# Attention and FFN on one core: three shared PSUM banks, normalising on VectorE, one output step per batch, new engine orders, and q, k, v as three float32r products

## The reference, cut to what matters

```python
xn = layernorm(x)                                   # x: 8 batches x 256 tokens x 256
kqv = xn @ Wqkv + bqkv                              # 16 heads of 16
scores = einsum('bsnh,btnh->bnst', k, q) / 4        # triu kept, -10000 below the diagonal
attn = softmax(scores, axis=2)
out = einsum('bnkq,bknh->bqnh', attn, v) @ Wo + bo
x_qdq = fp8(clip(xn / s_in, -448, 448)) * s_in
ffn = x_qdq @ (w_fp8 * w_scale).T
result = x + out + ffn                              # float32
```

## Time and profile before

| | us |
|---|---|
| median of 2 runs | 283.17 (281.4 and 284.94) |
| the profiled execution, its own time | 286.0 |
| its span, first to last instruction | 284.3 |
| TensorE matmuls busy | 205.1 (72%) |
| VectorE, ScalarE, GpSimd busy | 139.2, 104.1, 155.1 |
| mean granted TensorE clock | 0.862 of 2.4 GHz |

### The profile page before, as it was taken

How to read it: one execution, slowest core, us unless ns; L and a number is a source line. 1 busy time by engine, 2 the same in 40 slices (tenths; PEclk the granted TensorE clock), 3 DMA queues, 4 the chain that set the end, 5 groups by cost and what they waited for, 6 DMA issues and landing times.

```text
span 284.3 us, 4678 instructions
## 1 busy us (share of the span) xinstructions
PE 205.1 (72%) x1668; PEld 154.0 (54%) x1668; DVE 139.2 (49%) x265; ACT 104.1 (37%) x171; POOL 155.1 (55%) x352
## 2 busy tenths in 40 slices
PE   5196633847886597968785779766987869958945
PEld 5175532636755285746463656655765646635613
DVE  3836832567766144747671164529454743421220
ACT  4122300323530444246424434154416524635410
POOL 7472394496482866458737936386627433443320
PEclk9997965865995977999999697999799986986977
DMA  6619939759282006520661025703370010010011
GB/s 162 180 26 202 200 69 158 207 95 122 59 140 36 0 0 113 101 58 1 111 117 40 2 60 96 112 0 68 71 127 2 5 39 0 6 37 0 2 37 37
DMA packets 24444, 20.59 MB, mean 72 GB/s; under 512 B 2589, under 2 KB 24166, under 8 KB 24422
## 3 DMA queue, kind: packets, MB, share of 16 engines
q1 hardware_dynamic: 23024, 19.18, 35.9%
q10 hardware_dynamic: 1398, 1.12, 1.5%
HBM read 3.22 MB, written 2.10 MB: 19 GB/s over the span
## 4 chain that ended last, share of the span: by engine, by line
PE 51%; DVE 19%; POOL 14%; issue 8%; ACT 6%; DMA 1%; DVEq 0%; POOLq 0%; ACTq 0%
PE bankB L917 8%; PE ps L864 6%; PE bankA L978 5%; DVE row_max L661 5%; PE pso L889 5%; POOL xn L258 4%; ACT probs L473 3%; POOL probs L387 3%; PE bankB L924 3%; PE ps L847 2%; PE ps L843 2%; PE ps L849 2%; PE pso L895 2%; PE bankB L907 2%; PE bankA L924 2%
## 5 line engine op out<-in xcount | busy, mean ns | idle before, releaser
L661 DVE TENSOR_REDUCE row_max<-ps 128x4 f32<-128x1024 f32 (+1 forms) x48 | 58.5, 1221 | 64.7 <-PE ps L849 35.9
L387 POOL TENSOR_SCALAR_AFFINE_SELECT probs<-probs 128x256 f32<-128x256 f32 x128 | 49.1, 413 | 49.9 <-ACT probs L473 49.7
L473 ACT ACTIVATE probs<-ps 128x1024 f32<-128x1024 f32 x48 | 49.1, 1023 | 18.3 <-PE ps L864 13.8
L864 PE MATMUL ps<-q_stack,k_stack 99*128 99x256 bf16 x128 | 23.9, 319 | 11.6 <-ACT probs L473 11.6
L405 POOL TENSOR_TENSOR y<-y,x_all 128x256 f32<-128x256 f32 x16 | 11.2, 724 | 33.9 <-ACT y L528 33.9
L917 PE MATMUL bankB<-xT,wqk_sb 128*128 128x256 f32 x64 | 22.4, 511 | 8.0 <-ACT xs L522 7.9
L847 PE MATMUL ps<-k_stack,q_stack 96*128 96x128 bf16 x128 | 21.4, 244 | 6.5 <-DVE row_max L661 6.3
L864 PEld LDWEIGHTS ps<-q_stack,k_stack 99*128 99x128 bf16 x128 | 13.1, 113 | 18.6 <-ACT probs L473 14.6
L917 PEld LDWEIGHTS bankB<-xT,wqk_sb 128*128 128x128 f32 x64 | 16.3, 267 | 11.8 <-issue 7.3
L849 PE MATMUL ps<-k_stack,q_stack 125*128 125x128 bf16 x128 | 21.4, 243 | 0.0
L495 ACT ACTIVATE o_raw<-pso 128x512 f32<-128x512 f32 x16 | 9.6, 597 | 27.9 <-PE pso L895 27.9
(11 more groups left out here) (132 smaller groups left out, 391.8 us busy)
## 6 DMA issues: line engine op xcount, KB each, us to landing
q_stack<-q_parts SPq DMA_DIRECT2D x48, 128.0 KB
k_stack<-k_parts SPq DMA_DIRECT2D x48, 128.0 KB
x_all<-in_L_attn_x_dram SPq DMA_DIRECT2D x8, 256.0 KB, 5.7
out_dram<-y SPq DMA_DIRECT2D x8, 256.0 KB, 2.1
k_stack<-fixed_k SPq DMA_DIRECT2D x4, 256.0 KB, 5.4
q_stack<-fixed_q SPq DMA_DIRECT2D x4, 256.0 KB, 6.0
wqkv_sb<-in_L_attn_Wqkv_dram ACTq DMA_DIRECT2D x3, 256.0 KB, 4.0
wo_sb<-in_L_attn_Wo_dram ACTq DMA_DIRECT2D x1, 256.0 KB, 4.3
```

The lines of the kernel that those rows point to most:

```text
L387: ins = pool.affine_select(out=v[:, h:h + 2], in_=v[:, h:h + 2], compare_op=ALU.is_ge, fill=0.0, base=0, pattern=[[0, 2], [1, P]], channel ...
L473: act.activation(probs[:, i, :], ps2[:], ACT.Exp, scale=SCALE).then_inc(exp_done, 1)
L661: dve.tensor_reduce(dst, src, AX_X, ALU.max).then_inc(max_done, 1)
L864: mm = pe.matmul(ps2[:, h * S:h * S + S], k_stack[0:K_SOFT, s, hh, 0:P], q_stack[0:K_SOFT, s, hh, :], start=True, stop=True)
```

## The change

- **Banks.** A third shared bank C, made free because `pso` shrinks from two banks to one (both halves use it in turn). A table gives each result its bank: transposed x in C, q in A, k in C, v in A, suffix sums in A, maxima in C, the two halves of o and the normalised o in B, FFN in C, the projected output in A.
- **Normalising** (`norm`) goes from GpSimd to VectorE. The inverse root of the first three groups (batches 0 to 4) starts from ScalarE's square root and takes four VectorE instructions; the last group (batches 5 to 7) keeps the 14 on GpSimd.
- **float32r.** The weights and x are cut into a float32r part and a float32r rest, and each of q, k and v is the sum of rest times part, part times rest, and part times part: 12 TensorE products of 128x256 for each of q, k, v and batch, where 4 float32 products (8 instructions) were. The weights are cut on ScalarE and GpSimd before the loop; x is cut by ScalarE (`xT_out`) and a new VectorE instruction (`xT_low`, 128x512), for which the projections wait.
- **One end of a batch.** `divide_o`, `transpose_norm_o` and `oT_out` run once a batch for both halves.
- **Orders.** All five engines' lists are written anew; the loop's are below. The bias parts move from VectorE to GpSimd, `split` of batch 0's q too. `xs` gets three buffers. y and the weights share memory, as oT and the FFN weight's steps do.

```diff
+BANK = {"xT": "C", "q": "A", "o1": "B", "k": "C", "suffix": "A", "norm": "B", "max": "C", "v": "A", "o0": "B",
+        "ffn": "C", "proj": "A"}
...
+            if g < ROOTS:
+                eng.wait_ge(root_ready, g + 1)
+                then(eng.reciprocal(r, std[:, lo:hi]))
...
@@ SP @@
             load_x(1)
+            sp.wait_ge(fixed_ready, 1)
+            load_fixed(0)
             load_x(2)
             load_x(3)
-            sp.wait_ge(fixed_ready, 1)
-            load_fixed(0)
+            load_x(4)
...
@@ GpSimd @@
+                if j == 3:
+                    pool.wait_ge(wqk_ready, 1)
+                    for k in range(KT):
+                        ins = pool.tensor_tensor(wqk_lo[:, k].rearrange("p (m d h) -> p m d h", m=2 * KT, d=HD),
...
-                if p < B:
-                    norm(p)
                 causal(n, 0)
+                causal(n, 1)
+                if p < B:
+                    split(pool, p, "q", 2)
+                causal(n, 2)
                 if p - 1 < B:
                     round_x(p - 1)
...
+                if n == 0:
+                    inverse_std(pool, 3)
+                if n == 0:
+                    residual(0)
+                    residual(1)
...
@@ ScalarE @@
+            root(0)
             act.wait_ge(wqk_landed, 2 * 16)
...
                     exponentials(n, 4)
-                    if n + 1 < B:
-                        ffn_out(n + 1, "A")
-                    if p < B:
-                        values_out(p)
+                if p < B:
+                    values_out(p)
+                if live:
                     exponentials(n, 5)
+                if f < B:
+                    ffn_out(f)
...
@@ VectorE @@
+            def norm(b):
+                wait(dve, xT_mm, b - 1)
...
+            def xT_low(b):
+                dve.wait_ge(xT_ready, b + 1)
+                wait(dve, v_mm, b - 1)
+                dve.tensor_tensor(xT_lo[:, b % 2], bank[BANK["xT"]][:].rearrange("p (k s) -> p k s", k=KT),
+                                  xT_hi[:, b % 2].bitcast(F32), ALU.subtract).then_inc(xT_lo_ready, 1)
...
+                if p < B:
+                    norm(p)
                 if f < B:
                     maxima(f, 3)
-                if n in (0, 2):
-                    moments(3 + n // 2)
+                if p < B:
+                    xT_low(p)
                 if f < B:
                     maxima(f, 4)
...
                 if g < B:
                     maxima(g, 2)
+                if a >= 0:
+                    add_up(a)
...
@@ TensorE @@
-                    for k in range(KT):
-                        col = j * D + m * P
-                        mm = pe.matmul(dst[:, m * S:m * S + S], wqk_sb[:, k, col:col + P], xT[:, b % 2, k, :],
-                                       start=(k == 0), stop=(k == KT - 1))
+                    cols = slice(j * D + m * P, j * D + m * P + P)
+                    for n, (w, t) in enumerate(((wqk_lo, xT_hi), (wqk_hi, xT_lo), (wqk_hi, xT_hi))):
+                        for k in range(KT):
+                            mm = pe.matmul(dst[:, m * S:m * S + S], w[:, k, cols], t[:, b % 2, k, :],
+                                           start=(n == 0 and k == 0), stop=(n == 2 and k == KT - 1))
```

More of the change, by code:

```diff
@@ L18 @@
 F32 = mybir.dt.float32
+F32R = mybir.dt.float32r
 I32 = mybir.dt.int32
@@ L244, in then @@
                 eng.wait_ge(rstd_step[g], step[0])
+            if g < ROOTS:
+                eng.wait_ge(root_ready, g + 1)
+                then(eng.reciprocal(r, std[:, lo:hi]))
+                then(eng.scalar_tensor_tensor(out=a, in0=v, scalar=-0.5, in1=r, op0=ALU.mult, op1=ALU.mult))
+                then(eng.tensor_tensor(a, a, r, ALU.mult))
+                then(eng.scalar_tensor_tensor(out=r, in0=a, scalar=1.5, in1=r, op0=ALU.add, op1=ALU.mult))
+                return
             eng.wait_ge(moments_ready, g + 1)
@@ L319, in _ @@
             other_parts(1)
+            max_to_stack(0)
+            load_x(5)
+            first_parts(2)
             load_fixed(2)
[L321 to L324, removed]
             other_parts(2)
+            load_x(6)
+            load_x(7)
             load_fixed(3)
@@ L555, in _ @@
             xs_out(1)
-            part0(1, "q", "B")
-            part0(1, "k", "A")
+            part0(1, "q")
+            root(2)
+            part0(1, "k")
+            act.activation(warm[:], var_eps[:, 0:1], ACT.Exp, scale=-1.0)
+            act.wait_ge(bias_mm, 1)
+            act.activation(ob[:, 1], pso[0:PARTS, 0], ACT.Copy).then_inc(ob_ready, 1)
             values_out(1)
@@ L683, in rest1 @@
                 for m in range(KT):
-                    ins = dve.scalar_tensor_tensor(out=rest[qk][:, m, :], in0=bank[bk][:, m * S:m * S + S],
+                    ins = dve.scalar_tensor_tensor(out=rest[qk][:, m, :], in0=bank[BANK[qk]][:, m * S:m * S + S],
                                                    scalar=b_col[:, KT * j + m:KT * j + m + 1],
@@ L713, in add_up, with divide_o @@
-            def add_up(b, bk):
+                src = bank[BANK[f"o{half}"]][:].rearrange("p (t h e) -> p t h e", t=TB, h=HALF)[:, :, :, 0:NVC]
+                heads = slice(HALF * half, HALF * half + HALF)
+                dve.tensor_tensor(o_sum[:, :, heads], src, o_masked[:, b % 2, :, heads], ALU.add).then_inc(norm_step, 1)
+            def divide_o(b):
+                dve.wait_ge(norm_step, 4 * b + 2)
+                dve.reciprocal(o_den[:], o_sum[:, :, :, HD]).then_inc(norm_step, 1)
+                dve.wait_ge(norm_step, 4 * b + 3)
+                wait(dve, oT_mm, b)
+                dve.tensor_tensor(o_tok[:].rearrange("p t (h d) -> p t h d", d=HD), o_sum[:, :, :, 0:HD],
+                                  o_den[:].unsqueeze(3).to_broadcast([P, TB, H, HD]), ALU.mult).then_inc(norm_step, 1)
@@ L876, in values @@
                 if j == 0:
-                    wait(pe, o_raw_ready, 2 * (b - 1) + half + 1)
+                    if b == 0 and half == 0:
+                        pe.wait_ge(ob_ready, 1)
+                    wait(pe, o_raw_ready, 2 * b + half)
                     pe.wait_ge(v_ready, b + 1)
-                    if b == 0:
-                        pe.wait_ge(w8T_ready, 1)
                 s = b % STACKS
@@ L988, in _ @@
             pe.transpose(ps1[:, 2 * KT:3 * KT], bv_row[:], ident[0:KT, 0:KT]).then_inc(b_mm, 1)
-            pe.wait_ge(wqk_ready, 1)
-            project_qk(0, "q", "B")
-            project_qk(0, "k", "A")
-            pe.wait_ge(wv_landed, 16)
-            project_v(0, "B")
-            transpose_x(1, "B")
-            project_qk(1, "q", "B")
-            project_qk(1, "k", "A")
-            project_v(1, "B")
+            pe.wait_ge(wqk_lo_ready, 1)
+            project_qk(0, "q")
+            project_qk(0, "k")
+            pe.wait_ge(wv_lo_ready, 1)
+            project_v(0)
+            transpose_x(1)
+            project_qk(1, "q")
+            pe.wait_ge(b_col_ready, 1)
+            project_qk(1, "k")
+            pe.wait_ge(bv_ready, 1)
+            pe.wait_ge(wo_landed, 16)
+            for k in range(KT):
+                mm = pe.matmul(pso[0:PARTS, 0], bv_cols[:, k], wo_sb[:, k], start=(k == 0), stop=(k == KT - 1))
+            mm.then_inc(bias_mm, 1)
+            project_v(1)
+            phase1(0, 0)
+            transpose_x(2)
+            phase1(0, 1)
+            phase1(0, 2)
+            project_qk(2, "q")
+            phase1(0, 3)
+            phase1(0, 4)
+            phase1(0, 5)
+            project_qk(2, "k")
+            transpose_max(0)
+            phase1(1, 0)
+            project_v(2)
+            phase1(1, 1)
             pe.wait_ge(w8_ready, 1)
```

470 lines of the change are left out of this document (236 added, 234 removed).

## The result

The changed kernel takes 223.07 us (median of 2 runs, 222.35 and 223.79); the ratio to before is 0.7878, 95% interval [0.7639, 0.8116]. The profiled execution took 223.79, 222.1 of them its span, so 62.2 less than the one of before (286.0).

The account below looks back on a forecast made before the run. No engine fills a turn; a chain of waits sets its length, stretched by lower clock. Start 46, five turns 118.5, turns 5 and 6 35, tail 29.5 make 229, plus 1.7 outside the span 230.7: predicted 230, range 214 to 256.

Parts of the forecast that it names:

- start: Stretch before the loop's turns, up to phase2(0,0): forecast 46 us against 65.8 before, bounds 43 to 52.
- n = 0: First turn of the loop: 26.5 us, 4.0 of it for VectorE's moments, one clip and batch 0's FFN.
- n = 2 to 4: Third to fifth turns of the loop: 67.5 us together, 22.5 each.
- n = 5, 6: Last two turns, without a front end: 35 us against 39.6, 2.3 a turn less.
- tail: Stretch after the turns: 29.5 us against 30.3; joined division and transposes add 0.9, one wait is lost.
- The price of a float32r product: TensorE's q, k and v: 0.11 us a product, so 1.3 instead of 1.92 for each of q, k, v.
- Rivals 1 (0.24): TensorE's q, k, v: a float32r product takes 0.24 us, plus 20, 250 in all; chance 0.12.
- 3 (0.48): TensorE's q, k, v: a float32r product runs like a whole float32 product, 0.48 us; 305 in all, chance 0.04.
- (A) to (D): Four pieces of a full turn's chain of waits, cut at projection, v, q and batch g's first slot: 20.0 against 26.7.
- The allowance of 2.5 a turn: Added to a turn's 20.0 for what does not fit on VectorE and for lower clock: 22.5.
- rival 2: VectorE and GpSimd hold each other up more: 4 a turn and 2 in the opening stretch, 252; chance 0.11.
- the 1.4 allowed: VectorE's two normalising instructions each wait for one GpSimd instruction of 0.7: 1.4 us a turn, inside the 2.5.

Follow-up runs that it names:

- the edit that takes GpSimd out of the chain: Changed kernel with round_x moved to the head of GpSimd's turn, ahead of the first mask: 221.01 us, ratio 0.7849, turns 20.5.

## Why the prediction was right

The time (230 forecast, 223.07) lies inside the range. By its own steps, forecast against the profiled execution (223.8), it is 6.9 off; 4.2 too little in the start and 11.1 too much elsewhere partly cancel, so some of its closeness is luck:

| step | forecast | measured | off |
|---|---|---|---|
| start | 46 | 50.2 | +4.2 |
| n = 0 | 26.5 | 26.2 | -0.3 |
| n = 1 | 24.5 | 22.8 | -1.7 |
| n = 2 to 4 | 67.5 | 62.7 | -4.8 |
| n = 5, 6 | 35 | 33.5 | -1.5 |
| tail | 29.5 | 26.7 | -2.8 |

**The price of a float32r product** held: 0.116 against 0.11. Rivals 1 (0.24) and 3 (0.48) are out. But what it is worth is small: the run with float32 has shorter turns (20.5), and only where GpSimd is out of the way does float32r win 0.6 a turn. The subtraction, 0.69 as forecast, eats most of what a turn's three groups save (0.25 to 0.3 each).

**The turn's line** held: (A) to (D) 20.0, measured 20.5 once GpSimd is out of the chain. In that run it took 5.5 from v to the projection's end (forecast 5.3), from there to q 4.3 (4.7), from q to the next v 10.7 (10.0). The last part runs another way than I wrote: not through k and the suffix but through maxima(f,5), the split of the maxima and the division on VectorE, for which the transposes wait. That the sum came so near is in this part luck.

**The allowance of 2.5 a turn** was mis-sized, and it is the largest part of the miss: 0.9 instead of 2.5, 4.8 in n = 2 to 4. It was for the lower clock and for VectorE; the clock stayed at 1.00 from n = 2 to n = 6, and VectorE, as full as I said (16.5), did not bind by its sum. What bound was not in the prediction at all: GpSimd's ring, 20.9, of which I made no sum. It costs 0.4 above the line. Two lines within 0.4 us are why the edit that takes GpSimd out of the chain gained 0.4 a turn and no more, and it made n = 1 longer.

**VectorE and GpSimd** do hold each other up, less than rival 2 said in a turn: normalising took 1.10 beside GpSimd's masks instead of 0.74, 0.4 of the 1.4 allowed. In the start it is larger: 3.00 for batch 1 beside the clearing of v_sb (2.35), 5.24 in the run with float32. The Trainium skill (SBUF — State Buffer, § Who interferes with whom) says that a VectorE instruction in a two-port mode and one of GpSimd lock each other out for a whole instruction. In the run with float32 the second of the two normalising instructions agrees: it took 2.79 beside the clearing, which kept its 2.35. The first agrees only in part: it and the select beside it both took 2.53, and one side that waits for the other does not make both long. Yet taking normalising off GpSimd was worth more than it cost: 3.0 to 3.3 a turn in the changed kernel (with the lower clock of that run in it), 2.1 on the mean in the kernel before.

**The start** failed by 4.2. q of batch 0 started at 11.36, as forecast (11.3 to 13.4), after GpSimd's 2.98 for the weights' rests. The step that failed is the landing of batch 0's stack: 32.6 instead of 29.5. Its last block was issued 2.0 earlier than before, as forecast, but took 8.28 to land; in the changed kernel run again it landed at 31.2. Issued 1.15 earlier still, behind more loads of x, it landed no earlier. From 25 to 35 us the DMA engines were busy throughout in both kernels (shares of 1.13 to 1.21), but they moved 156 to 157 GB/s in the changed kernel, 178 to 192 in it run again, and 199 to 201 in the kernel before; what sets that rate no run shows. The rest is what follows the landing: 17.5 to phase2(0,0) instead of 16.5.

**n = 0** held by luck: its 4.0 were for VectorE's work, but what TensorE waited for at its end, 3.73 us, was batch 1's maxima, 24 KB that took 8.65 us to land. They were issued at 67.66, behind a fixed block (landed at 69.75) and half a stack of batch 3; x6 and x7 had landed by 66.83. **The tail** and n = 5, 6 came out 2.8 and 1.5 shorter than my terms; no run was made on them, so the cause stays open.

## What to carry to other kernels

After a rewrite of all orders, add up the line of every engine around a turn, its waits included, not just the two that look full: the one that closed this turn was busy for 76% of it. When two lines stand within 2% of each other, as here, an edit on one is worth only that 2%, and the floor is the busiest engine's own work. An order moved on the producer gained nothing here (21.9) until the consumer's list was moved with it (20.8). And a steady turn is not the whole run: look at the first turns too before an order is called better.

## What the runs showed of the hardware

An instruction as small as 128x2 can be held on VectorE for whole instructions of GpSimd: in the run with SP's loads earlier

```profile
12.28 4.50 DVE L687 TENSOR_SCALAR var_eps<-mean_var 128x2 f32<-128x2 f32 x1
```

beside GpSimd's rest of the v weights (1.27) and its clearing (2.35); with the clearing cut to 0.54 and 0.20 the same addition still took 2.60. And at a granted clock of 0.50 (1.2 GHz) the tail's last projection, eight float32 instructions, takes 3.73 where eight took 1.92 at 1.00; in the 7.9 us before it TensorE was at work for 4.84:

```profile
214.99 3.73 PE bankA L1060 x8
```
